# Building the expert lists inside the experts' program, with the moving operand of the slot products stored token column first

## The reference

```
x = x + 0.5 * ffn(layernorm(x))        # 16 experts of 512 tokens each, chosen by the expert, + shared expert
x = x + attn_moe(layernorm(x))         # linear attention with gates, then the mixture below
x = x + 0.5 * ffn(layernorm(x))

probs = softmax(xf @ router_W + router_b)             # 8 experts
topk_probs, topk_idx = top_k(probs, 2); topk_probs /= topk_probs.sum(-1)
for eid in range(8):
    idx = the first 1280 (token, choice) pairs with topk_idx == eid, in order of the token
    h = gelu(xf[tok] @ W1[eid] + b1[eid]) @ W2[eid] + b2[eid]
    out = out.at[tok].add(gate[:, None] * h)
```

## Time and profile before

| | us |
|---|---|
| three runs | 2413.36, 2414.99, 2411.85 |
| median | 2413.36 |
| profiled execution, its own time | 2413.13 |
| its span, first to last instruction | 2411.3 |
| mean granted clock of TensorE, share of full speed | 0.959 |
| TensorE busy | 2251.1 (93%) |
| VectorE busy | 1651.4 (68%) |
| ScalarE busy | 906.2 (38%) |
| GpSimd busy | 870.5 (36%) |

### The profile page before, as it was taken

How to read it: one execution, slowest core, us unless ns; L and a number is a source line. 1 busy time by engine, 2 the same in 40 slices (tenths; PEclk the granted TensorE clock), 3 DMA queues, 4 the chain that set the end, 5 groups by cost and what they waited for, 6 DMA issues and landing times. The chain is left out here.

```text
span 2411.3 us, 37963 instructions
## 1 busy us (share of the span) xinstructions
PE 2251.1 (93%) x13564; PEld 1952.4 (81%) x13564; DVE 1651.4 (68%) x3584; ACT 906.2 (38%) x1703; POOL 870.5 (36%) x916
## 2 busy tenths in 40 slices
PE   6998999999998799955999999977998999999998
PEld 5887888888887577743899999976887888888887
DVE  5776777777776566554666666745775777777775
ACT  5222333333332666631233333325222333333332
POOL 4201333333332777722144444434201333333232
PEclk9998999999999899975999999998998999999999
DMA  5003454444442311122144344434003454445452
GB/s 178 27 27 123 109 142 124 133 112 142 123 133 52 133 34 36 34 59 58 45 83 84 85 84 85 82 60 154 27 27 121 112 141 124 133 112 143 123 133 45
DMA packets 154107, 228.04 MB, mean 95 GB/s; under 512 B 33344, under 2 KB 104512, under 8 KB 153920
## 3 DMA queue, kind: packets, MB, share of 16 engines
q1 hardware_dynamic: 102656, 157.62, 20.5%
q0 software_dynamic: 39936, 55.93, 13.3%
q10 hardware_dynamic: 11328, 12.07, 1.5%
HBM read 171.16 MB, written 54.39 MB: 94 GB/s over the span
## 5 line engine op out<-in xcount | busy, mean ns | idle before, releaser
L1166 ACT ACTIVATE me_act_f<-me_in,me_bias 128x512 f32<-128x512 f32 (+1 forms) x192 | 119.1, 620 | 303.3 <-PE me_in L142 274.5
L1166 ACT ACTIVATE f1e_silu<-f1e_in,f1e_bias 128x512 f32<-128x512 f32 (+1 forms) x136 | 90.1, 663 | 341.3 <-PE f1e_in L142 293.3
L1166 ACT ACTIVATE f2e_silu<-f2e_in,f2e_bias 128x512 f32<-128x512 f32 (+1 forms) x136 | 90.1, 663 | 340.9 <-PE f2e_in L142 293.2
L140 PE MATMUL f2e_in<-f2e_xt_hi,f2e_w_hi 128*128 128x512 f32 (+1 forms) x544 | 208.6, 383 | 3.9 <-DVE f2e_xt_lo L1228 2.3
L140 PE MATMUL f1e_in<-f1e_xt_hi,f1e_w_hi 128*128 128x512 f32 (+1 forms) x544 | 208.6, 383 | 3.8 <-DVE f1e_xt_lo L1228 2.3
L142 PE MATMUL f2e_in<-f2e_xt_hi,f2e_w_lo 128*128 128x512 f32 (+1 forms) x544 | 207.7, 382 | 0.0
L142 PE MATMUL f1e_in<-f1e_xt_hi,f1e_w_lo 128*128 128x512 f32 (+1 forms) x544 | 207.7, 382 | 0.0
L141 PE MATMUL f2e_in<-f2e_xt_lo,f2e_w_hi 128*128 128x512 f32 (+1 forms) x544 | 207.4, 381 | 0.0
L141 PE MATMUL f1e_in<-f1e_xt_lo,f1e_w_hi 128*128 128x512 f32 (+1 forms) x544 | 207.3, 381 | 0.0
L140 PE MATMUL me_down<-me_w_hi,me_act_hi 128*128 128x256 f32 x640 | 183.7, 287 | 0.0
L141 PE MATMUL me_down<-me_w_lo,me_act_hi 128*128 128x256 f32 x640 | 180.1, 281 | 0.0
(11 more groups left out here) (459 smaller groups left out, 6977.1 us busy)
## 6 DMA issues: line engine op xcount, KB each, us to landing
f_raw<-in_ffn_w SPq DMA_DIRECT2D x256, 384.0 KB
m_raw<-in_moe_w SPq DMA_DIRECT2D x64, 256.0 KB
f1s_x_all<-in_x SPq DMA_DIRECT2D x8, 512.0 KB, 5.9
after_ffn<-f1s_out SPq DMA_DIRECT2D x8, 512.0 KB
after_moe<-ma_x_all SPq DMA_DIRECT2D x32, 128.0 KB, 1.7
m_h<-ma_h SPq DMA_DIRECT2D x32, 128.0 KB, 1.7
f2s_x_all<-after_moe SPq DMA_DIRECT2D x8, 512.0 KB, 8.9
out<-f2s_out SPq DMA_DIRECT2D x8, 512.0 KB
```

The lines of the kernel that those rows point to most:

```text
L140: pe.matmul(out, lh, rh, start=first, stop=False, skip_group_check=True)
L1166: act.activation(dst[:, st % 2, 0:n], ps_in[st % 2][0][:, 0:n], func, bias=bias[:, b, f:f + 1]).then_inc(silu_done, 1)
```

## The change

- `make_lists` and its program are gone. A class `Lists` holds the same work in parts that `run_experts` calls at the head of its streams. It uses PSUM tiles of `run_experts` (`me_in` for the prefix products, `me_turn` for the slots).
- The constants and the router's bias are loaded by `attention`, on ScalarE's queue, two more loads there. The constant operations go to GpSimd and one to ScalarE.
- On VectorE the gates are computed behind the one-hot planes. The scan reads PSUM directly. Then come the splits of four weight slices, then the ids of expert 0 alone, then those of experts 1 to 3. The gathers of expert 0 (all ten tiles from one place) wait for the gates in DRAM and for the ids of expert 0; TensorE's first turn waits for all placed ids.
- Only two pairs of expert 0 are turned at the head. Expert 0 runs group by group as the last one does, its other pairs are turned at its steps 3, 4 and 6, those of expert 1 at steps 9 to 17 (before 13 to 21), and the first weight slices of expert 1 are converted at steps 19 to 22.
- The second lists are made within expert 1, not expert 0. Scatter ids are made for each half apart.
- `moved` is stored as [token column, row, expert] and no longer [row, expert, token column]: the product reads 160 neighbours, and VectorE writes with a step of 160 elements.

The core of the diff:

```diff
@@ class Planes
-        self.row_hot, self.moved = (scope.sb(n, [P, self.R, 4, T], F16) for n in ("row_hot", "moved"))
+        self.row_hot, self.moved = scope.sb("row_hot", [P, self.R, 4, T], F16), scope.sb("moved", [P, T, self.R * 4], F16)
     def move(self, dve, r0, r1):
-        return dve.tensor_tensor(self.moved[:, r0:r1].rearrange("p r f t -> p (r f) t"),
+        return dve.tensor_tensor(self.moved[:, :, r0 * 4:r1 * 4].rearrange("p t x -> p x t"),
                                  self.row_hot[:, r0:r1].rearrange("p r f t -> p (r f) t"),
                                  self.token[:].unsqueeze(1).to_broadcast([P, (r1 - r0) * 4, T]), ALU.mult)
     def products(self, pe, slots, t0, t1):
         for t in range(t0, t1):
-            ins = pe.matmul(slots, self.hot[:, :, :, t].rearrange("p f l -> p (f l)"), self.moved[:, :, :, t],
+            ins = pe.matmul(slots, self.hot[:, :, :, t].rearrange("p f l -> p (f l)"), self.moved[:, t, :],
...
+class Lists:
...
+    def sync(self, sp):
+        sp.dma_start(self.first.ident[:], self.consts[:, C_IDENT:C_IDENT + P]).then_inc(self.ident_in, 16)
+        for r in range(RAW_RING):
+            sp.dma_start(self.first.raw[:, r], self.expert_w[r]).then_inc(self.first.raw_in[r], 16)
+        sp.wait_ge(self.gate_shown, 1)
+        sp.dma_start(self.h_rows[:, D:D + self.E].rearrange("(t p) e -> p t e", p=P), self.shown[:]
+                     ).then_inc(self.gate_stored, 16)
+    def gpsimd(self, pool):
...
+        pool.wait_ge(self.gate_stored, 16)
+        pool.wait_ge(self.ids_done, 1)
+    def tensor(self, pe):
...
+        pe.wait_ge(self.moved_done, 1)
+        pe.wait_ge(self.hot_done, 1)
+        self.planes.products(pe, self.ps_slots, 0, T).then_inc(self.slots_done, 1)
+        pe.wait_ge(self.placed, 1)
+    def vector_planes(self, dve):
...
+        own.step(planes.rows_hot(dve, 0, 0, planes.R))
+        planes.move(dve, 0, planes.R).then_inc(self.moved_done, 1)
+        planes.lanes_hot(dve, 0, 0, planes.LANES).then_inc(self.hot_done, 1)
+        share = self.share
+        dve.wait_ge(self.gate_ready, 1)
...
+    def vector_place(self, dve):
+        dve.wait_ge(self.slots_done, 1)
+        self.planes.place(dve, self.ps_slots, 0, self.gather_ids, (0,)).then_inc(self.ids_done, 1)
+        self.planes.place(dve, self.ps_slots, 0, self.gather_ids, (1, 2, 3)).then_inc(self.placed, 1)
@@ run_experts
+    FIRST_AT, NEXT_AT = {3: 2, 4: 3, 6: 4}, {9: 0, 11: 1, 13: 2, 15: 3, 17: 4}
+    FREED = {(C - 1) * F_T + LAG + 1 + f: f for f in range(AHEAD)}
+        def by_group(e):
+            return e == E - 1 or planes and e == 0
-            return (st % F_T, st // F_T) if e == E - 1 else (st // n, st % n)
+            return (st % F_T, st // F_T) if by_group(e) else (st // n, st % n)
@@ tensor
+            if planes:
+                lists.tensor(pe)
+            for i in range(2):
+                turn(0, i)
             for st in range(LAG):
-                if st < C:
-                    for i in range(CH[st][0] // 2, CH[st][1] // 2):
-                        turn(0, i)
                 into(0, st, 0)
-            for i in range(CH[min(LAG, C) - 1][1] // 2, NI):
-                turn(0, i)
...
+                    if planes and e == 1:
+                        second_lists(st)
                     if planes and e == 0:
-                        second_lists(st)
-                    if st in ITEM_AT and left:
+                        if st in FIRST_AT:
+                            turn(0, FIRST_AT[st])
+                        if st in NEXT_AT:
+                            turn(1, NEXT_AT[st])
+                    elif st in ITEM_AT and left:
                         turn(e + 1, ITEM_AT[st])
@@ vector
-            low_part(0, 0)
-            for i in range(NI):
-                split_rows(0, i, 0)
-            gates(0, 0)
-            for f in range(1, AHEAD):
-                low_part(0, f)
+            if planes:
+                lists.vector_planes(dve)
+                for f in range(AHEAD):
+                    low_part(0, f)
+                lists.vector_place(dve)
+                for i in range(2):
+                    split_rows(0, i, 0)
@@ attention
-        N_CONST = 7
+        N_CONST = 9
-                             (norm2[:], w["norm2"]), (router_raw[:], w["router"])):
+                             (norm2[:], w["norm2"]), (router_raw[:], w["router"]), (cst[:], consts),
+                             (rb[:], w["router_b"].to_broadcast([P, MOE_E]))):
                 act.dma_start(dst, src).then_inc(const_in, 16)
```

More of the change, by code:

```diff
@@ L745, in products, with place @@
         for t in range(t0, t1):
-            ins = pe.matmul(slots, self.hot[:, :, :, t].rearrange("p f l -> p (f l)"), self.moved[:, :, :, t],
+            ins = pe.matmul(slots, self.hot[:, :, :, t].rearrange("p f l -> p (f l)"), self.moved[:, t, :],
                             start=(t == 0), stop=(t == T - 1), skip_group_check=True)
         return ins
-    def place(self, dve, slots, g, gather_ids):
+    def place(self, dve, slots, g, gather_ids, experts):
         out = gather_ids[:].rearrange("p (g f) j -> p g f j", f=4)[:, g]
         slots = slots.rearrange("p (j q) f -> p j q f", q=4)
-        for f in range(4):
+        for f in experts:
             for q in range(4):
@@ new lines, in scatter_ids @@
+    def scatter_ids(self, dve, own, g, gather_ids, scatter_ids):
+        of = slice(4 * g, 4 * g + 4)
+        idf, tmp, slot_no = self.idf[:, of], self.tmp[:, of], self.slot_no[:, of]
+        own.step(dve.tensor_copy(idf, gather_ids[:, of]))
+        own.step(dve.tensor_tensor(tmp, slot_no, self.counts[:, of].unsqueeze(2).to_broadcast([P, 4, self.NT]), ALU.is_ge))
+        own.step(dve.scalar_tensor_tensor(tmp, slot_no, float(N - N // 2), tmp, ALU.add, ALU.mult))
+        own.step(dve.tensor_tensor(idf, idf, tmp, ALU.add))
+        return dve.tensor_copy(scatter_ids[:, of], idf)
@@ L996, in _ @@
         def _(sp):
+            if planes:
+                lists.sync(sp)
             def one(e, b, left):
@@ L1032, in scatter_tile @@
                                         ).then_inc(last_landed if is_last(e, j) else scattered, 16)
-            if NT > FIRST_TILES:
+            if planes:
+                lists.gpsimd(pool)
                 take_ids(gid, gather_ids, 0)
-                for j in range(FIRST_TILES, NT):
+                for j in range(NT):
                     gather_tile(j)
+                pool.wait_ge(lists.placed, 1)
             rows_free(0)
@@ L1310, in second_lists @@
                     listing.at(1)
[L1311 to L1318 removed]
+                    planes.scatter_ids(dve, listing, 1, gather_ids, scatter_ids).then_inc(lists_done, 1)
+            if planes:
+                lists.vector_planes(dve)
[4 more added lines that the diff above has]
+                    split_rows(0, i, 0)
+            else:
+                low_part(0, 0)
+                for i in range(NI):
+                    split_rows(0, i, 0)
+                gates(0, 0)
+                for f in range(1, AHEAD):
+                    low_part(0, f)
             for st in range(LAG):
@@ L1321, in _ @@
                 next_slice(0, st, 1)
-            first = own.n
-            PER = NI + S * (2 if gated else 1)
             def one(e, b, left):
-                own.at(e * PER + first)
                 for st in range(LAG, steps(e)):
                     activate(e, st, b)
-                    if planes and e == 0:
+                    if planes and e == 1:
                         second_lists(st)
+                    if planes and e == 0 and st == 7:
+                        lists.vector_scatter(dve)
                     add_chunk(e, st - LAG, b)
@@ L1359, in ffn, with attention @@
         run_experts(nc, tag + "e", FFN_E, NT, True, ffn_w, ffn_b, ffn_db, consts, h_rows, acc, ids, ids,
-                    first.for_experts(), last, ends_program)
-def attention(nc, tag, x_in, acc, w, consts, norm2, logits, h_rows, spare, last):
+                    first, last, ends_program)
+def attention(nc, tag, x_in, acc, w, consts, norm2, cst, rb, logits, h_rows, spare, last):
     Q = T // BATCH
```

291 lines of the change are left out of this document (140 added, 151 removed).

## The result

The changed kernel takes 2429.38 us (median of 4 runs, 2426.93 to 2432.09) where the kernel before takes 2412.61 (4 runs): ratio 1.0069, 95% interval 1.0055 to 1.0084. It is 16.8 us slower, where 2402.0 was forecast, and the time lies above the whole range. The rival *The writes are worse than any row* is what came, at 4.37 ns per element where it had reckoned with 3.4. The profiled run took 2429.47, its span 2427.7.

A forecast was written before the change was run, and what follows sets the result against it. It took some 75 us before the first expert as latency, TensorE as the bound after 1137 us. Terms -20.2 + 1.5 + 1.15 + 3.2 + 1.0 + 1.2 + 1.0 = -11.15 against 2413.13 gave 2402, range 2392 to 2411.

The forecast's parts named there:

- The writes are worse than any row: Rival on VectorE's move: gain gone at 2.8 ns per element; at 3.4, 2419 us, slower than before; chance 0.1.
- The moved plane: VectorE's move in the first list, written with a step: 1.7 ns per element, 8.9 us instead of 2.83, +6.1.
- the second list: Lists made within expert 1: two moves of 4.5 instead of 1.49, +6.1; products 4.3 instead of 8.6; net +1.2.
- One element per cycle: Rival on VectorE's move: it only loses its doubled rate, 1.1 ns per element, 2395.5; chance 0.26 together with nothing lost.
- Front of the lists: VectorE's chain up to the row one-hots: bias wait, constants, gate arithmetic and small operations leave it, -4.9.
- Slot products: TensorE's 32 products of the first list, with adjacent columns: 0.15 each, 4.8 us instead of 9.2, -4.4.
- From the slots to the first product: Gate store ends last, by 1 us; first gather 1099.9, first turn 1104.0, first product 1110.0; full rate as if from 1112.0.
- its last rival: Gathers ahead of expert 0 wait for all experts' ids or the weight loads (1 MB): 2404 to 2408; beyond 2408, shared chance 0.14.
- Expert 0's order: Group-by-group walk of expert 0: turns inside the stream +1.5, table load +1.15, stop at step 17 +3.2, lower clock +1.0.
- The order of expert 0 eats the gain: Rival: VectorE late at turns of steps 9 to 15, TensorE's clock drops twice, 6 to 7 more, 2409; shared chance 0.14.
- The attention's start: Two more loads issued by ScalarE stand ahead of its first copy, on which TensorE's first work hangs: +1.0.

The follow-up runs named there:

- Experiment 3: Changed kernel with the loops of the move swapped: it writes neighbours and reads the one-hots with a step of 64 bytes; 2406.75 us, ratio 0.9974 to before.
- the probe: Kernel before with fifteen timed VectorE operations of 128x2560 elements at its head, varying steps and types; its own time says nothing.
- experiment 5: Changed kernel with one-hots stored row, token, expert, so the move writes runs of four 2-byte elements; 2397.98 us, ratio 0.9942 to before.
- experiment 8: Changed kernel with runs of four, earlier turns of expert 1's pairs, second products a step later, and gates ahead of the lane one-hots; 2396.87 us.
- experiments 1: Changed kernel with only the old layout of the moved plane put back (row, expert, token); 2402.85 us, ratio 0.9960 to before.
- 5 to 8: Changed kernel with runs of four (2397.98), then added in turn: earlier turns of expert 1's pairs (2397.07), later second products (2395.55), gates ahead of lanes (2396.87 us).
- experiment 9: Kernel before with a second set of timed VectorE operations at its head and GpSimd copies beside the last of them; its own time says nothing.

## Why the prediction was wrong, point by point

The ledger of the two profiles, in us of the span against before; the third column is what the runs showed.

| step | forecast | measured |
|---|---|---|
| ahead of the last logits | +1.0 | +0.3 (1061.88 - 1061.61) |
| front of the lists, to the row one-hots | -4.9 | -4.7 |
| first move | +6.1 | +19.5 |
| end of the move to the first product | -7.4 | -6.4 (22.45 against 28.86) |
| first product to the third stage | -6.0 | +8.6 (525.26 against 516.61) |
| third stage, its code unchanged | 0 | -0.9 (777.6 against 778.5) |
| sum | -11.2 | +16.4 |

(-7.4 is the forecast's 1110.0 less 1088.5, against 28.86; -6.0 is its other terms behind the first product.)

**The moved plane** is the step that failed, in two rows. I priced the stepped write of 2-byte elements by the stepped write of 4-byte elements, 1.7 ns, and closed the range at TensorE's 1.83. It is 4.37. The trace of before had no row of such a write, and the two rows that I took for bounds do not bound it: one was a 4-byte write, the other a read by TensorE. The same wrong price was used for **the second list**, +6.1 for two moves, and there it made stops of 21.94 us where "9 to 10" were forecast. Experiment 3, with moves of 8.7 and 4.57, has 9.02 there (2.98 and 6.04), 5.6 more than before, so the +6.1 was near for the moves that I had assumed. Put together: 13.5 in the first list, and in the second 12.9 of stops (21.94 - 9.02); what remains of the 27.6 between forecast and profile is 1.2, or 2.1 without the third stage. With 4.37 in place of 1.7 ns the forecast's own sum gives 2402 + 10,240 x 2.67 ns = 2429.3. That this meets the 2429.38 measured is partly luck: the smaller misses below have both signs, and runs of one kernel lie up to 6 us apart (2408.99 to 2414.99).

**The rivals.** *The writes are worse than any row* had the right step and a break-even of 2.8 ns, and got 0.1. What I held against it, that the f32 row jumps as well and pays only 0.64 more, is just what the probe refutes: the type of the output decides (4.46 against 11.29). *One element per cycle* is not what this write does, but it is what runs of four do: 5.49 us for the move in experiment 5, and a median of 2397.98 where that rival had 2395.5.

**Front of the lists**: right, -4.7 for -4.9.

**Slot products**: a little better than forecast: 4.11 for 4.8, and 2.35 + 1.33 for 4.3 in the second list.

**From the slots to the first product**: the gate store does end last, by experiment 8. The first gather came 7.9 us behind the lanes (1113.33 - 1105.41), 8.1 forecast. What I had too short is the way from the first gather to the first turn: 5.5 (1118.81 - 1113.33) where I took 4.1 from the bytes' landing. The rows suggest why. In the changed kernel the 1 MB of weight loads stands behind the gate store in SP's queue, and the DMA share is 0.93 to 1.07 from 1113 to 1117, just when the gathers run. In experiments 1 and 8 the loads are ahead of the gathers, the DMA share behind the first gather is under 0.5, and the same way takes 4.30 and 4.31 us. The prediction named this in its last rival and gave it no term of its own; no run moves the loads alone.

```profile
1112.29 0.19 POOL L1019 COPY me_gid<-m_ids 128x10 uint32<-128x10 uint32 x1 [47.03 <-DMA m_h<-me_shown]
1113.33 1.12 POOL L1022 DMA_INDIRECT m_rows<-m_h,me_gid  x1 [0.84 <-POOL me_gid L1019]
```

**Expert 0's order**: 1.14 for 1.15 at the table load, 3.06 for 3.2 at step 17, and behind it the lower clock as feared: products of 128x256 take 0.42 from 1187.80 and 0.32 at 1191.00, 0.28 before. Not foreseen were stops of 0.56, 0.49 and 1.14 in front of turns. Of the 6 to 7 us of the rival *The order of expert 0 eats the gain* about 2 came: those three stops are 2.2 together (2.2 in experiment 3 too), and experiment 3 is 1.8 longer than forecast between its first product and the third stage. A clock that drops twice, as the rival had it, did not come: the granted clock was 1.00 from 1130 to 1186 us, and 0.50 only behind the stop at step 17.

**The attention's start**: 0.3 instead of 1.0. The two runs were 0.55 apart the other way when the attention stage began (their ScalarE rows from 256 us on), so against that it is 0.8. In experiments 1, 3 and 5 to 8 the same subtraction gives 0.65 to 1.15, so the +1.0 was about right.

## What to carry over

Before transposing a plane in an elementwise operation, look at the bytes that each jump of the output writes: a lone 2-byte element in a product cost 4.4 ns here, a lone 4-byte one 1.8, and 2-byte elements in runs of two, four or eight 1.1 each. Put a small axis innermost on both sides (four experts here) and the transpose costs 5.49 us instead of 22.37 (2.83 with no transpose at all), with the reader's good layout kept. Where the trace has no row of an operation, rows of another type or another engine are no bounds: price the break-even, and if a factor of two in the unknown reaches it, its side needs more than one chance in ten.

## What was not expected of the hardware

- The same code ran with another granted clock from run to run. In the first stage, 180 to 185 us, the trace of before and that of experiment 3 show:

```profile
180.00:185.00 5.00, 5.00 (x31) 4.29 (x30) 3.22 (x17) 0.60 (x1) 0.00 (x0) 1.00 0.19 69
```

```profile
180.00:185.00 5.00, 5.00 (x25) 4.71 (x24) 1.05 (x2) 0.00 (x0) 0.00 (x0) 0.50 0.00 0
```

  TensorE is busy throughout in both, at 2.4 GHz in the one and 1.2 GHz in the other, and experiment 3's run is 4.9 us late from there on. What sets it the traces do not show. This is why stretches and stages, not spans, are compared above, and why kernels that differ by 1 or 2 us can't be ranked.
- GpSimd is held for as long as VectorE's stepped product runs. In the changed kernel a scatter request that takes 1.58 took 12.21 and the next one 11.03, just beside the two moves:

```profile
1207.60 1.58 POOL L1035 DMA_INDIRECT after_moe<-me_out,me_sid  x1 [0.30 <-issue]
1210.79 12.21 POOL L1035 DMA_INDIRECT after_moe<-me_out,me_sid  x1 [0.30 <-issue]
...
1224.80 11.03 POOL L1035 DMA_INDIRECT after_moe<-me_out,me_sid  x1 [0.30 <-issue]
```

  With the short moves of experiment 5 (2.82 us) the same two requests took 4.07 and 3.02.
  The Trainium skill (SBUF — State Buffer, SBUF: two separate sides) says that the pair of ports which the two engines share is an exclusive lock, held for a whole instruction, also by a VectorE operation with two inputs against a GpSimd one that reads. The trace agrees: the copy of 0.40 us took 11.00 in experiment 9, and its VectorE operation 11.26.
- A slot product with adjacent columns takes 0.128 us at the lower clock and 0.083 (1.33 / 16) at the full one, against 0.29 at either with stepped columns (9.21 / 32 and 4.75 / 16 before).
